# Attention on one core: other PSUM banks for scores and maxima, value products in pairs of key tiles, and another split of the softmax sums

## What is computed

```python
h = rmsnorm(x, g1) * (1 + scale1) + shift1
q, k, v = split(h @ w_qkv + b_qkv); q, k = rope(q), rope(k)
attn = softmax(q @ k.T / sqrt(32))            # per batch and head, 2048 x 2048
x = x + (attn @ v) @ w_ao + b_ao
h = rmsnorm(x, g2) * (1 + scale2) + shift2
x = x + swiglu(h @ w_fc + b_fc) @ w_fo + b_fo
```

## Time and profile before

| | |
|---|---|
| median of 3 runs | 3562.36 us (3561.84 to 3563.03) |
| the profiled execution | 3560.96 us |
| its span, from the first to the last instruction | 3558.8 us |
| TensorE busy | 3200.1 us, 90% |
| VectorE busy | 1938.6 us, 54% |
| GpSimd busy | 1739.5 us, 49% |
| ScalarE busy | 1530.7 us, 43% |
| mean granted TensorE clock | 0.946 |
| HBM traffic | 76 GB/s over the span |

### The profile page before, as it was taken

One profiled execution on the slowest core, in us unless ns is written; L12 is line 12 of the kernel. 1 busy time (PEld: TensorE's weight loads), 2 busy tenths in 40 slices (PEclk: granted clock), 3 DMA queues, 4 the chain that ended last, 5 costly groups with the idle time before them and its releaser, 6 DMA issues. The chain is left out here.

```text
span 3558.8 us, 53024 instructions
## 1 busy us (share of the span) xinstructions
PE 3200.1 (90%) x15180; PEld 2062.1 (58%) x15180; DVE 1938.6 (54%) x3062; ACT 1530.7 (43%) x2784; POOL 1739.5 (49%) x796
## 2 busy tenths in 40 slices
PE   5999699999899989999899994443999997999999
PEld 5777444444444444444444442333888886888887
DVE  2666487787678767787687773434322121322222
ACT  1333046676676756777577672332211111211111
POOL 0555348888688877888688886563000000100000
PEclk9999779999999999999999997766999999999999
DMA  4455549898788978898798986655311211411210
GB/s 169 146 161 161 153 97 200 178 199 174 167 192 177 195 155 184 186 191 192 151 196 172 197 187 156 193 161 177 130 48 61 81 48 63 142 55 47 94 48 24
DMA packets 178300, 508.05 MB, mean 143 GB/s; under 512 B 24891, under 2 KB 42411, under 8 KB 144943
## 3 DMA queue, kind: packets, MB, share of 16 engines
q0 software_dynamic: 36240, 248.53, 34.3%
q1 hardware_dynamic: 131284, 233.58, 21.9%
q10 hardware_dynamic: 10512, 22.81, 1.9%
HBM read 175.18 MB, written 93.62 MB: 76 GB/s over the span
## 5 line engine op out<-in xcount | busy, mean ns | idle before, releaser
L737 DVE TENSOR_REDUCE b_mpart<-b_m 128x1 f32<-128x512 f32 x2136 | 1325.8, 683 | 401.2 <-PE b_m L787 397.1
L676 ACT ACTIVATE b_pt<-b_s 128x512 f32<-128x512 f32 x2048 | 1113.9, 596 | 521.1 <-PE b_s L812 465.4
L715 POOL TENSOR_TENSOR b_acc<-b_acc,b_pt 128x2048 f32<-128x2048 f32 x225 | 1047.1, 4654 | 169.8 <-DMA b_pt<-b_pt 168.3
L812 PE MATMUL b_s<-b_qs,b_ks 98*128 98x512 f32 x2050 | 890.4, 434 | 42.4 <-ACT b_pt L676 41.9
L787 PE MATMUL b_m<-b_ks,b_qs 96*128 96x512 f32 x2136 | 785.7, 414 | 20.8 <-issue 20.5
L812 PEld LDWEIGHTS b_s<-b_qs,b_ks 98*128 98x128 f32 x2050 | 386.4, 188 | 693.0 <-ACT b_pt L676 641.1
L864 PE MATMUL b_o<-b_pt,b_vg 128*32 128x512 f32 x4096 | 548.0, 607 | 0.0
L787 PEld LDWEIGHTS b_m<-b_ks,b_qs 96*128 96x128 f32 x2136 | 416.6, 195 | 95.4 <-DVE b_mpart L737 26.3
L1249 DVE SCALAR_TENSOR_TENSOR d_uf<-d_a,keep_chan,d_sg 128x512 f32<-128x512 f32 x128 | 96.1, 751 | 577.7 <-PE d_a L1277 577.7
L1201 POOL DMA_DIRECT2D d_raw<-in_w_fc x32 | 23.9, 754 | 586.9 <-POOLq L1126 495.8
L1220 ACT ACTIVATE d_sg<-d_g,keep_chan 128x512 f32<-128x512 f32 x128 | 88.0, 688 | 419.8 <-PE d_g L1277 419.8
(11 more groups left out here) (127 smaller groups left out, 3411.8 us busy)
## 6 DMA issues: line engine op xcount, KB each, us to landing
b_pt<-b_pt POOLq DMA_DIRECT2D x225, 1024.0 KB, 8.0
b_ks<-scratch_qk_hi SPq DMA_DIRECT2D x36, 512.0 KB, 5.3
b_qs<-scratch_qk_hi SPq DMA_DIRECT2D x68, 256.0 KB, 5.8
scratch_qk_hi<-a_q_hi SPq DMA_DIRECT2D x64, 256.0 KB
scratch_qk_lo<-a_q_lo SPq DMA_DIRECT2D x64, 256.0 KB
d_h_hi<-scratch_h_hi SPq DMA_DIRECT2D x16, 1024.0 KB, 7.4
d_h_lo<-scratch_h_lo SPq DMA_DIRECT2D x16, 1024.0 KB, 9.7
d_y<-scratch_y SPq DMA_DIRECT2D x16, 1024.0 KB, 8.1
```

What stands on the lines that cost most here:

```text
L676: act.activation(pt[:, kt % RING, h, :], ps_s[:, i % LEAD, :], ACT.Exp, scale=SCALE).then_inc(p_ready, 1)
L715: pool.tensor_tensor(acc[slot][:], acc[slot][:], pt[:, (2 * n + 3) % RING, :, :], ALU.add).then_inc(pool_added, 1)
L737: dve.tensor_reduce(mpart[slot][:, i // 4, i % 4:i % 4 + 1], ps_m[:, i % EARLY, :], AX.X, ALU.max).then_inc(max_done, 1)
L812: pe.matmul(ps_s[:, i % LEAD, :], ks[kslot][0:QR, h, kt * P:(kt + 1) * P], qs[qslot][0:QR, h, :], start=True, stop=True).then_inc(st_done, 1)
```

## The change

PSUM: the scores get three banks (`LEAD` = 3) in place of two, and the bank `ps_d` goes. The softmax sums are now made in one of the score banks, at a place in the rotation that is counted in (`score_place`, `SUMS_AT` = 27), and the transposed maxima in one of the four banks of maxima (`maximum_bank`, `TURN_AT` = 3). The transpose comes after the third maximum of step 10.

TensorE: the value products come after every odd tile, for two tiles together; the orders of scores and maxima are `smsmsmms` in even and `msmsmsms` in odd steps. The sums of the unit before are made after step 5 in place of 7, from two terms: `acc` and the exponentials of tile 15, which GpSimd no longer adds.

GpSimd: `PAIRS` is 6, `ADDS` stays 8. Tile 14 is added alone, with no transfer (`add_single`). The queue in a unit is: tile 14 of the unit before, its last pair's sum, first pair, transfer 0, and for n from 1 to 5 transfer n and the sum of pair n-1. At the start, four slots of `pt` are set to one, in place of two.

ScalarE and VectorE wait and read to match: ScalarE copies the sums ahead of score 27 and the products behind score 4 (they were behind tile 8 and behind score 1), and waits for `d_ps` before it writes tile 7 over tile 15.

```diff
@@ -466,11 +466,23 @@
-PAIRS = NK // 2 - 1
-ADDS = PAIRS + 1
+PAIRS = NK // 2 - 2
+ADDS = PAIRS + 2
 RING = 8
-LEAD = 2
+LEAD = 3
 EARLY = 4
+TURN_AT = 3
+SUMS_AT = 4 * 6 + LEAD
+def score_place(i):
+    return i + (i >= SUMS_AT)
+def maximum_bank(n, place):
+    return (65 * (n % 8) + place) % EARLY
 def stage_b(nc, io, keep, scratch):
@@ -499,7 +511,7 @@
         dcol = m.sb("dcol", [P, GH * TB // P])
-        ps_s, ps_m, ps_o, ps_d = m.ps("s", LEAD), m.ps("m", EARLY), m.ps("o", 1), m.ps("d", 1)
+        ps_s, ps_m, ps_o = m.ps("s", LEAD), m.ps("m", EARLY), m.ps("o", 1)
@@ -515,15 +527,16 @@
-        ORDER, TURN = "smsmmsms", 10
+        ORDER, TURN = ("smsmsmms", "msmsmsms"), 10
...
         AHEAD = PER * (NK - TURN)
-        assert ORDER.count("m") == PER and ORDER.count("s") == GH
-        D_AT = 7
+        assert all(o.count("m") == PER and o.count("s") == GH for o in ORDER)
+        D_AT = 5
+        assert SUMS_AT == GH * (D_AT + 1) + LEAD
         def added(u, n):
-            return ADDS * u + ADDS + (n + 3 if n < PAIRS - 1 else 2 + ADDS)
+            return ADDS * u + ADDS + (n + 4 if n < PAIRS - 1 else 2 + ADDS)
@@ -647,13 +660,17 @@
             def read_denominators(u):
...
                 act.wait_ge(d_out, 16 * (u + 1))
-                act.activation(d_sb[:], ps_d[:, 0, :], ACT.Copy).then_inc(d_read, 1)
+                act.activation(d_sb[:], ps_s[:, SUMS_AT % LEAD, :], ACT.Copy).then_inc(d_read, 1)
             def slot_free(u, kt, pair, j):
...
                 old = (kt - RING) % NK
-                if old >= 2 and old % 2 == 0:
+                if old == NK - 1:
+                    act.wait_ge(d_ps, u + 1 + 1)
+                elif old == NK - 2:
+                    act.wait_ge(pool_added, ADDS * u + ADDS + 1)
+                elif old >= 2 and old % 2 == 0:
@@ -661,8 +678,8 @@
                     act.wait_ge(pool_added, added(u if kt >= RING else u - 1, old // 2 - 1))
-                else:
-                    act.wait_ge(pool_added, ADDS * u + ADDS + 1)
+                elif kt >= RING:
+                    act.wait_ge(pool_added, ADDS * u + ADDS + 3)
@@ -672,13 +689,13 @@
                         i = GH * kt + h
+                        if i == SUMS_AT:
+                            read_denominators(u)
                         act.wait_ge(st_done, STEPS * (u + 1) + i + 1)
-                        act.activation(pt[:, kt % RING, h, :], ps_s[:, i % LEAD, :], ACT.Exp,
+                        act.activation(pt[:, kt % RING, h, :], ps_s[:, score_place(i) % LEAD, :], ACT.Exp,
                                        scale=SCALE).then_inc(p_ready, 1)
-                        if kt == 0 and h == LEAD - 1:
+                        if i == GH:
                             read_products(u)
-                    if kt == D_AT + 1:
-                        read_denominators(u)
@@ -689,9 +706,9 @@
             pool.wait_ge(ones_in, 32)
-            pool.memset(pt[:, RING - 2:RING, :, :], 1.0).then_inc(ones_ready, 1)
+            pool.memset(pt[:, RING - 4:RING, :, :], 1.0).then_inc(ones_ready, 1)
             pool.wait_ge(ones_ready, 3)
-            pool.dma_start(pt[:, RING - 1, :, :], pt[:, RING - 2, :, :], accum_op=ALU.add).then_inc(pair_in[1], 16)
+            pool.dma_start(pt[:, RING - 3, :, :], pt[:, RING - 4, :, :], accum_op=ALU.add).then_inc(pair_in[1], 16)
...
             def first_pair(u, slot):
@@ -714,16 +731,23 @@
                 pool.tensor_tensor(acc[slot][:], acc[slot][:], pt[:, (2 * n + 3) % RING, :, :], ALU.add).then_inc(pool_added, 1)
+            def add_single(u, slot):
+                pool.wait_ge(p_ready, STEPS * (u + 1) + GH * (NK - 1))
+                pool.wait_ge(pool_added, added(u, PAIRS - 2))
+                pool.tensor_tensor(acc[slot][:], acc[slot][:], pt[:, (NK - 2) % RING, :, :], ALU.add).then_inc(pool_added, 1)
             def body(u, pair, j):
+                add_single(u - 1, (j + 1) % 2)
+                add_pair(u - 1, j - 1, pair, PAIRS - 1, (j + 1) % 2)
...
                 fold_pair(u, j, pair, 0)
-                add_pair(u - 1, j - 1, pair, PAIRS - 1, (j + 1) % 2)
...
             run(pool, body)
-            pool.sem_inc(pool_added, 1)
+            add_single(UNITS - 1, 1)
@@ -731,20 +755,22 @@
             dve.sem_inc(mlo_ready, 1)
-            def maxima(n, slot, lo, hi):
+            def maxima(n, j, lo, hi):
                 for i in range(lo, hi):
+                    at = maximum_bank(j, i + (i >= TURN_AT))
                     dve.wait_ge(max_ps, ITEMS * n + i + 1)
-                    dve.tensor_reduce(mpart[slot][:, i // 4, i % 4:i % 4 + 1], ps_m[:, i % EARLY, :], AX.X, ALU.max).then_inc(max_done, 1)
+                    dve.tensor_reduce(mpart[j % 2][:, i // 4, i % 4:i % 4 + 1], ps_m[:, at, :], AX.X, ALU.max).then_inc(max_done, 1)
             def finish_max(n, slot):
...
                 dve.tensor_reduce(mneg[:], mpart[slot][:], AX.X, ALU.max, negate=True).then_inc(mneg_ready, 1)
-            def split_max(n):
+            def split_max(n, j):
+                at = maximum_bank(j + 1, TURN_AT)
                 dve.wait_ge(mT_ps, n + 1)
-                dve.tensor_copy(m_hi[:], ps_d[0:GH * SUB, 0, 0:P]).then_inc(mhi_ready, 1)
+                dve.tensor_copy(m_hi[:], ps_m[0:GH * SUB, at, 0:P]).then_inc(mhi_ready, 1)
                 dve.wait_ge(mhi_ready, n + 1)
-                dve.tensor_tensor(m_lo[:], ps_d[0:GH * SUB, 0, 0:P], f32(m_hi[:]), ALU.subtract).then_inc(mlo_ready, 1)
+                dve.tensor_tensor(m_lo[:], ps_m[0:GH * SUB, at, 0:P], f32(m_hi[:]), ALU.subtract).then_inc(mlo_ready, 1)
             def invert(u):
@@ -752,23 +778,18 @@
             finish_max(0, 0)
-            maxima(1, 1, 0, PER)
-            split_max(0)
-            maxima(1, 1, PER, AHEAD)
+            maxima(1, 1, 0, TURN_AT)
+            split_max(0, 0)
+            maxima(1, 1, TURN_AT, AHEAD)
             def body(u, pair, j):
-                at = AHEAD
-                for kt in range(NK):
-                    if kt == TURN:
-                        finish_max(u + 1, (j + 1) % 2)
-                        at = 0
-                    ahead = 1 if kt < TURN else 2
-                    maxima(u + ahead, (j + ahead) % 2, at, at + PER)
-                    at += PER
-                    if kt == TURN + 1:
-                        split_max(u + 1)
-                    if kt == NK - 2:
-                        invert(u)
+                maxima(u + 1, j + 1, AHEAD, ITEMS)
+                finish_max(u + 1, (j + 1) % 2)
+                maxima(u + 2, j + 2, 0, TURN_AT)
+                split_max(u + 1, j + 1)
+                maxima(u + 2, j + 2, TURN_AT, AHEAD - PER)
+                invert(u)
+                maxima(u + 2, j + 2, AHEAD - PER, AHEAD)
@@ -779,21 +800,28 @@
             pe.sem_inc(st_done, STEPS)
-            def maxima(n, kslot, qslot, lo, hi):
+            def maxima(n, j, kslot, qslot, lo, hi):
...
                     h, s, k = i // 16, i // 4 % 4, i % 4
-                    pe.wait_ge(max_done, ITEMS * (n + 1) + i + 1 - EARLY)
-                    pe.matmul(ps_m[:, i % EARLY, :], qs[qslot][0:KR, h, s * P:(s + 1) * P],
+                    place = i + (i >= TURN_AT)
+                    if place == TURN_AT + EARLY:
+                        pe.wait_ge(mlo_ready, n + 1)
+                    else:
+                        last = i - EARLY + (TURN_AT < place < TURN_AT + EARLY)
+                        pe.wait_ge(max_done, ITEMS * (n + 1) + last + 1)
+                    pe.matmul(ps_m[:, maximum_bank(j, place), :], qs[qslot][0:KR, h, s * P:(s + 1) * P],
...
             def denominators(u, slot):
                 pe.wait_ge(pool_added, added(u - 1, PAIRS - 1))
-                pe.wait_ge(mlo_ready, u + 2)
-                pe.wait_ge(d_read, u + 1)
-                for h in range(GH):
-                    last = pe.matmul(ps_d[h * HD:(h + 1) * HD, 0, :], ones[:, 0:HD], acc[slot][:, h, :], start=True, stop=True)
+                pe.wait_ge(p_ready, STEPS * (u + 1))
+                terms = [acc[slot][:]] + [pt[:, n % RING, :, :] for n in (NK - 1,)]
+                for n, term in enumerate(terms):
+                    for h in range(GH):
+                        last = pe.matmul(ps_s[h * HD:(h + 1) * HD, SUMS_AT % LEAD, :], ones[:, 0:HD], term[:, h, :],
+                                         start=n == 0, stop=n == len(terms) - 1)
...
             def operands(j, pair):
@@ -801,26 +829,31 @@
                 pe.wait_ge(k_in[j // 4 % 2], 96 * (pair + j // 8 + 1))
-            def turn_max(n):
+            def turn_max(n, j):
                 pe.wait_ge(mneg_ready, n + 1)
-                pe.transpose(ps_d[0:GH * SUB, 0, 0:P], mneg[:], ident[:]).then_inc(mT_ps, 1)
+                pe.transpose(ps_m[0:GH * SUB, maximum_bank(j + 1, TURN_AT), 0:P], mneg[:], ident[:]).then_inc(mT_ps, 1)
             def scores(n, kslot, qslot, i):
                 kt, h = i // GH, i % GH
-                pe.wait_ge(p_ready, STEPS * (n + 1) + i + 1 - LEAD)
```

(43 more changed lines are left out.)

## The result

The changed kernel takes 3587.11 us (median of 6 runs, 3580.68 to 3598.83), the kernel before 3562.70 (6 runs, 3559.12 to 3563.35): ratio 1.0073, 95% interval 1.0062 to 1.0083. It is slower by 24 us, where 9 us faster was forecast. Its runs also lie 18 us apart, against 4 before. Beside the last two experiments stand further runs of the kernel before, of which one took 10148.05 us and is left out of every median here.

A forecast was written before the change was run, and what follows sets the result against it. After the change GpSimd's closed chain (51.6 us a unit) would bind over TensorE (49.7): four passes of 407.0 against 409.5 give -10, the last unit's later sums make it -8.5, so 3553 from the 3562.36 median; range 3512 to 3600.

The forecast's parts named there:

- What bounds now: Attention units: TensorE binds before at 50.8 us; after the change GpSimd at 51.6 takes its place over TensorE's 49.7.
- GpSimd's closed chain: GpSimd's queue over one unit: six sums of 4.53 (27.2 us) and three waits for transfers (24.4), together 51.6.
- One sign: GpSimd's timeline after the change: it would wait for landings after transfers 0, 2 and 4, and for products never late in a pass.
- the sum of the three waits: GpSimd's waits for transfers 0, 2 and 4 in a unit: mean 24.4 us, bounds three of 7.0 to three of 9.2.
- transfer 4: GpSimd's adding transfer beside the load of step 2 and the reciprocals: wait taken as 8.8, 8.8, 8.0, 7.7 by unit.
- The prediction's own formula for a pass: Pass of 8 units: 8 x 49.7 + 3.1 slow start + (7 x 1.9 - 7.0 slack) = 407.0 us, against 409.5 before.
- TensorE's unit: TensorE's own work per unit: 8 x 5.85 + 2 x 0.86 + 0.1 + 0.6 + 0.5 = 49.7 us (48.8 to 50.8).
- Rival A: TensorE binds after all: GpSimd's waits fall to 7.0 to 7.5, its chain to about 49; 3527 us, chance 0.27.
- Rival B: Late GpSimd issues transfers 0 and 1 together; collisions lengthen the waits to 26.0, chain to 53.2; 3598 us, chance 0.25.
- Rival C: Pass changes: a hidden GpSimd restart of 12 us leaves it 6 us late in three passes; 3571 us, chance 0.06.
- Rival D: TensorE's pairing of products saves nothing, since 0.33 and 0.35 are waits, not breaks; unit 51.7, 3600 us, chance 0.02.
- The tail: End of the last unit: its sums end 1.7 us later behind its products than before the change.

The follow-up runs named there:

- the last two experiments: Key and value loads spread evenly, two in each unit: on the changed kernel 3580.74 us; with transfer 0 also issued ahead of the first pair's sum 3497.01 us.
- the swap: Changed kernel with transfer 0 of a unit issued ahead of the first pair's sum in GpSimd's queue: 3518.14 us, ratio 0.9867 to the kernel before.

## Why the prediction was wrong

**What bounds now: right.** GpSimd's closed chain took TensorE's place. It stands in the timeline link by link, and taking 4.53 out of it gave 69 us back, while adding 2.2 a unit to TensorE cost 10, inside the spread. One sign came otherwise: GpSimd does wait for products late in a pass, but ahead of transfer 1 and inside the wait for transfer 0.

**The step that failed** is the sum of the three waits, taken as 24.4 and measured 25.6. I worked it out again from the issue times of the changed kernel, as the time between transfers 0, 2, 4 and the next 0, less 4.53 for each sum between them. Left out are the first and the last unit of each pass; 24 units remain, and the rows are means:

| unit of the group | taken | measured (transfer 0 + 2 + 4) | chain measured |
|---|---|---|---|
| first (keys in steps 0, 1, 2) | 25.4 | 9.74 + 7.59 + 10.35 = 27.7 | 54.9 |
| second (keys in steps 0, 1, 2) | 25.4 | 8.44 + 8.34 + 9.87 = 26.7 | 53.8 |
| third (values in steps 0, 1) | 24.6 | 9.03 + 7.65 + 7.97 = 24.7 | 51.8 |
| fourth (no load) | 22.4 | 7.59 + 7.22 + 8.62 = 23.4 | 50.6 |

The mean is 25.6 and the chain 52.8, not 51.6; the prediction itself put the turning point at 52.0. The mis-sized term is above all transfer 4: 9.2 on average where 8.3 was taken, 0.9 of the 1.2, and most beside the load of step 2, taken as 8.8 and measured 9.9 and 10.3. The row at hand had 9.2 and I went below it, toward the middle of the bounds, though the change moves this transfer toward the unit's end: in units 4 and 12 it goes out 44.0 us into the unit, before 38.9 and 39.2, and the next unit's queries start at 50.8. The two loads in each unit show that the load makes some 2 us of this wait; why it is longer than in the row is not shown, and the queries are a guess. The prediction's own formula for a pass comes to 3.1 + 8 x 49.2 + 7 x (52.8 - 49.2) - 7.0 = 414.9 with the measured chain and TensorE's measured unit; 414.2 was measured. The mechanism was right and the sum of waits 5% too small, where each 0.1 us of the chain is worth about 3 us.

**TensorE's unit** was taken as 49.7 and is 49.2. A pair is 5.83 (5.85); the step with the transpose takes 6.34 and so costs 0.51 more (0.6 with the transpose itself); from the sums with their products, 1126.57 to 1130.14, comes 1.71 more than without (1.72). What is left for the products' copy is 0.3, where I had put 0.6. This miss of 0.5 a unit hardly counts, since TensorE does not bind. The sum for the whole kernel has a slip besides: -10 and 1.7 make -8.3, not -8.5, so 3554.

**Rival A** (TensorE binds) fell: the waits for transfers 0, 2 and 4, which it put at 7.0 to 7.5, are 8.7, 7.7 and 9.2 on average. The Trainium skill ("DMA: Bandwidth & Descriptors", Anatomy of one DMA) gives a transfer from GpSimd 2.0 us plus its bytes over 436 GB/s, so 4.4 for 1 MB by estimate; by that the chain would be 41 and TensorE would bind. The traces do not bear it out for these transfers, which also add: in none of the runs did one take under 6.9.

**Rival B** gave the nearest time (3598) and the nearest waits (26.0), but its mechanism is refuted: with transfer 1 issued within 1 us of it, transfer 0 still lands after 7.1 where no load runs, and with the load moved away it does so in the units with loads. Nor does transfer 1's tail hold up transfer 2: in unit 12 transfer 1 lands 14.5 after its issue, 1 us after transfer 2 has gone out, and transfer 2 is still back after 7.4. The waits are longer than taken, as B said, but not through these collisions, so that B's time came near is luck.

**Rival C** fell: the first transfer of the later passes goes out 12.9 to 13.1 us into the unit, as early as in the first pass (12.6), so GpSimd has caught up by then. **Rival D** fell with the 5.83.

**The tail** of the last unit: from the last copy at 2176.2, GpSimd's last sum ends at 2190.0, 13.8 later; before it was 12.5. Some 1.3, where 1.7 was forecast.

## What to carry to other kernels

When an engine with its own transfers is hidden by a small margin, write out its closed chain with the waits in it before you shorten the engine that hides it. Ask of each sum whether it lies inside a wait or outside; here the same eight sums, one of them on the other side of a transfer's issue, were 69 us. And take the price of a wait from the rows with the same neighbours at the new place; if the result turns on a few tenths, say that the sign is open.

## What the runs showed of the hardware

A stall of TensorE can be paid twice. In unit 5 of the changed kernel it waits 3.17 us for ScalarE, and then works at half its clock; the stretches' table and TensorE's timeline:

```profile
744.00:750.40 6.40, 6.08 (x32) 3.13 (x32) 3.78 (x7) 3.90 (x8) 6.32 (x2) 1.00 0.56 145
750.40:753.50 3.10, 0.02 (x1) 0.00 (x0) 1.51 (x3) 0.56 (x2) 3.10 (x2) 1.00 0.03 5
753.50:760.50 7.00, 6.91 (x27) 3.06 (x31) 2.08 (x3) 3.29 (x7) 4.62 (x2) 0.52 0.28 57
760.50:766.00 5.50, 5.50 (x32) 3.09 (x24) 3.03 (x6) 3.56 (x8) 1.42 (x2) 1.00 1.04 206
```

```profile
753.59 0.71 PE L845 MATMUL b_s<-b_qs,b_ks 98*128 98x512 f32 x1 [3.17 <-ACT b_pt L695]
...
756.78 3.64 PE L899 MATMUL b_o<-b_pt,b_vg 128*32 128x512 f32 x16
```

The granted clock goes from 1.00 (2.4 GHz) to 0.52, so 1.2 GHz for nearly all of the 7 us behind the hole; the two tiles' products take 3.64 and not 1.92. The length of a hole alone does not tell it: one of 1.43 ahead of 1380.96 was followed by a clock of 0.50 (1381.8 to 1385.2), one of 1.48 at 744.3 was not, nor was the one of 1.22 in unit 12.

Such stretches come 14 times in the changed kernel's attention, the pass changes not counted, and twice with the swap, in the same instructions. From first to last copy:

```profile
480.70:2176.20 1695.50, 1617.61 (x8732) 859.53 (x8730) 1278.86 (x2175) 1104.12 (x2112) 1317.54 (x445) 0.97 0.77 160
480.90:2111.90 1631.00, 1585.94 (x8732) 855.29 (x8731) 1275.76 (x2175) 1099.70 (x2112) 1328.13 (x446) 0.99 0.79 167
```

The first line is the changed kernel, the second the swap. Of the 64.5 us between them, 33 are TensorE's idle time and 32 are longer busy time for the same matmuls. So a TensorE that looks busier can be one that waits more. Still the slower clock is not what set the pace in the changed kernel: away from the first units of the passes none of the transfers 0, 2 and 4 waited for TensorE's products, so the slower clock did not hold up GpSimd's chain directly. What it adds at the pass changes, and by shifting the loads against the transfers, was not tried. The changed kernel's spread of 18 us between runs, and that of 5 with TensorE binding throughout, go with how a chain of transfers varies; that too is only seen beside it, not shown.
